# Reordering the tail of a mixture-of-experts stage: bias matmuls, sums' loads, residual chunks and a wait for key rows

## The reference

```
xn = layernorm(x); s = mixer_l(xn); g = silu(ffn_l(xn)); x = x + s * g
```

## Time and profile before

| what | value |
|---|---|
| runs before | 835.33, 833.63, 836.16 us; median 835.33 us |
| profiled execution | 835.67 us, of which the span is 833.9 us; mean granted TensorE clock 0.954 |
| busy, share of the span | PE 84%, DVE 77%, ACT 61%, POOL 47% |
| chain that ended last, by engine | PE 34%, DVE 22%, issue 18%, POOL 13%, ACT 10%, DMA 3% |

### The profile page before, as it was taken

The page is one execution under the profiler, slowest core; times in us unless marked ns, Lnnn a source line. Parts: engine busy times, 40 slices in busy tenths (PEclk is TensorE's granted clock), DMA queues, the critical chain, the costliest instruction groups (busy, mean ns, idle before and its releaser), DMA issues.

```text
span 833.9 us, 13257 instructions
## 1 busy us (share of the span) xinstructions
PE 702.1 (84%) x4706; PEld 352.3 (42%) x4720; DVE 643.3 (77%) x1290; ACT 507.6 (61%) x746; POOL 388.3 (47%) x385
## 2 busy tenths in 40 slices
PE   5996987989979977869999989994877888888986
PEld 2332453444446753334444444441323344444453
DVE  3988777888727745787989924489899999899995
ACT  4788645888865545626666653668454555555473
POOL 0000305686836652041000002028999999999962
PEclk9996997999999996987999999997999999999999
DMA  8600000000144119100000000305447444645441
GB/s 348 277 1 0 4 1 1 1 31 23 37 117 132 44 28 298 42 0 2 3 2 3 2 2 1 126 16 166 159 154 276 147 149 143 201 162 178 156 161 51
DMA packets 30433, 75.97 MB, mean 91 GB/s; under 512 B 4335, under 2 KB 14008, under 8 KB 29344
## 3 DMA queue, kind: packets, MB, share of 16 engines
q1 hardware_dynamic: 26048, 67.41, 23.7%
q0 software_dynamic: 4320, 7.72, 2.7%
HBM read 59.28 MB, written 17.01 MB: 91 GB/s over the span
## 4 chain that ended last, share of the span: by engine, by line
PE 34%; DVE 22%; issue 18%; POOL 13%; ACT 10%; DMA 3%; SPq 0%; DVEq 0%; POOLq 0%; ACTq 0%
POOL arena L2231 7%; PE ps L806 4%; DVE ttr_out L960 4%; DVE xq L960 4%; DVE arena L2156 3%; DVE band L2163 3%; POOL exp_in L2198 3%; PE ps L784 2%; PE ps L642 2%; PE ps L295 2%; PE ps L1448 2%; ACT arena L876 2%; PE ps L652 1%; PE ps L772 1%; PE ps L1215 1%
## 5 line engine op out<-in xcount | busy, mean ns | idle before, releaser
L2156 DVE TENSOR_TENSOR_SCAN arena<-ps,arena 128x1024 f32<-128x1024 f32 x64 | 146.6, 2291 | 18.5 <-ACT ps L2032 9.8
L876 ACT ACTIVATE arena<-ps 128x1024 f32<-128x1024 f32 x128 | 124.8, 1025 | 35.3 <-PE ps L795 25.8
L2032 ACT ACTIVATE ps<-arena,negA 128x1024 f32<-128x1024 f32 x64 | 71.5, 1118 | 102.0 <-DVE arena L2156 101.7
L1866 PE MATMUL ps<-band,w 128*128 128x512 f32 x256 | 120.1, 592 | 0.0
L2163 DVE TENSOR_TENSOR band<-arena,ps 128x1024 f32<-128x1024 f32 x64 | 76.6, 1196 | 2.3 <-PE ps L1751 2.3
L2231 POOL TENSOR_TENSOR arena<-arena,gate 128x1024 f32<-128x1024 f32 x32 | 75.6, 2366 | 4.3 <-DMA gate<-b_dram 3.4
L2231 POOL TENSOR_TENSOR arena<-arena 128x1024 f32<-128x1024 f32 x32 | 75.2, 2364 | 0.3
L806 PE MATMUL ps<-arena 128*32 128x256 f32 x1024 | 70.9, 397 | 1.0 <-ACT arena L876 1.0
L1751 PE MATMUL ps<-xq,sel 128*128 128x512 bf16 x115 | 35.7, 383 | 41.8 <-DVE band L2163 39.1
L1074 POOL COPY arena<-arena 128x128 f32<-128x128 f32 x32 | 8.4, 296 | 123.7 <-PE ps L806 107.2
L1866 PEld LDWEIGHTS ps<-band,w 128*128 128x128 f32 x256 | 48.6, 190 | 40.2 <-issue 30.6
(11 more groups left out here) (404 smaller groups left out, 1620.4 us busy)
## 6 DMA issues: line engine op xcount, KB each, us to landing
gate<-b_dram SPq DMA_DIRECT2D x32, 512.0 KB, 3.7
arena<-b_dram SPq DMA_DIRECT2D x32, 512.0 KB, 4.4
wf<-pack1f_dram SPq DMA_DIRECT2D x1, 3076.0 KB, 15.2
wf<-bias_rows SPq DMA_DIRECT2D x1, 3072.0 KB, 15.4
exp_in<-band SPq DMA_DIRECT2D x2, 1032.0 KB, 5.0
exp_out<-band SPq DMA_DIRECT2D x2, 1024.0 KB, 17.9
e_in<-band SPq DMA_DIRECT2D x2, 1024.0 KB, 21.7
arena<-e_out SPq DMA_DIRECT2D x4, 512.0 KB, 5.7
```

What stands on the lines that cost most here:

```text
L876: act.activation(probs[g % 2][:, 2 * pr:2 * pr + 2, :, :].rearrange("p h k n -> p (h k n)"), PAIRS[l][("S2", i, b)], ACT.Exp).then_inc(A[" ...
L1866: mm = pe.matmul(ps[:, j, :], ident, hc[i % 2][:, j * CH:(j + 1) * CH], start=False, stop=True, skip_group_check=True)
L2032: act.activation(dA_ps, dt3[:, cb, hf * HALF:(hf + 1) * HALF], ACT.Exp, scale=negA[:, cb * STATE + n:cb * STATE + n + 1]).then_inc(M["dA"], 1)
L2156: dve.tensor_tensor_scan(hst[i % 2], dA_ps, dbu[i % 4], 0.0, ALU.mult, ALU.add).then_inc(M["scan"], 1)
```

## The change

The bias matmuls move behind the last `down`. SP issues the four loads of the sums before it waits for `rows_ready`. DVE takes each residual two sums behind its own sum, so that the list reads sum 0, sum 1, sum 2, residual 0, sum 3, residual 1, residual 2, residual 3. In block 2's attention DVE's wait for all 256 of `k_rows` moves from before the order to each key eviction (before it stands a wait for 64, which block 1 has met). In block 3 the second early projection moves behind the logits.

```
-            dve.wait_ge(k_rows, 16 * HH * (1 if l == 1 else 4))
+            dve.wait_ge(k_rows, 16 * HH)
...
                     dve.wait_ge(*A.at("rep_ps", n + 1))
+                    dve.wait_ge(k_rows, 16 * HH * (1 if l == 1 else 4))
                     dve.tensor_tensor(k_st[:, g, c * CH:(c + 1) * CH], ...k_pat, ALU.add)
...
-                if j == N1:
-                    bias_from_table()
                 if 1 <= j <= N1:
                     turn(j - 1)
                 if j >= 2:
                     down(j - 2)
+            bias_from_table()
...
-            for c in range(NCH):
+            def sum_of(c):
                 dve.wait_ge(*MOE.at("y_in%d" % c, 16))
                 a_, b_ = (y1[k][:, 4 * c:4 * c + 4, :] for k in range(2))
                 dve.tensor_tensor(a_, a_, b_, ALU.add).then_inc(MOE["y_sum"], 1)
+            for c in range(NCH + 1):
+                if c < NCH:
+                    sum_of(c)
+                if c >= 2:
+                    residual_dve(dve, 1, ..., (c - 2,))
+            residual_dve(dve, 1, ..., (NCH - 1,))
...
                 if t == NT // 2:
                     project(0, 0, 0)
-                    project(1, 0, 1)
...
             mm.then_inc(M["lg"], 1)
+            project(1, 0, 1)
             project(2, 1, 0)
...
+            moe_sums(sp_)
             sp_.wait_ge(rows_ready, 1)
             sp_.dma_start(bias_rows..., rows_sb...).then_inc(rows_out, 16)
-            moe_sums(sp_)
             sp_.wait_ge(rows_out, 16)
...
             moe_dve(dve)
-            residual_dve(dve, 1, lambda c: chunk(s_sb, c), lambda c: [MOE.at("acc", c + 1)])
```

More of the change, by code:

```diff
@@ L1542, in moe_dve @@
                 dve.tensor_tensor(a_, a_, b_, ALU.add).then_inc(MOE["y_sum"], 1)
+            for c in range(NCH + 1):
+                if c < NCH:
+                    sum_of(c)
+                if c >= 2:
+                    residual_dve(dve, 1, lambda c: chunk(s_sb, c), lambda c: [MOE.at("acc", c + 1)], (c - 2,))
+            residual_dve(dve, 1, lambda c: chunk(s_sb, c), lambda c: [MOE.at("acc", c + 1)], (NCH - 1,))
         def moe_pool(pool):
```

## The result

The changed kernel takes 830.16 us (median of 12 runs, 828.12 to 835.03) against 835.4 us for the kernel before in the same runs: 0.9939, 95% interval 0.9925 to 0.9953. Run a second time it gave 0.9952 (0.9932 to 0.9971). So the change brings 4 to 5 us where 2.0 were forecast. Its profiled execution took 830.28 us with a span of 828.4 us, at a mean granted clock of 0.956.

What follows compares the result with a forecast made beforehand. Scatter, loads, sums and norm, then a later-ending DMA chain to the key rows, were taken as the bound. Gains of 1.1 (first key eviction) and 0.9 (projection) made 2.0 us: 833.7 profiled, 833.3 median, range 830.6 to 837.0.

Steps and rivals of the forecast that it cites:

- The two chains: Before block 2's key evictions: scatter, loads, sums, norm; and DMAs alone (bias write, `bias_q`, near tables, key rows), ending later.
- Bias matmuls behind the last tile: At the last expert tiles: the last scatter starts 1.36 us earlier, limited by POOL running scatters back to back.
- `rows_ready` and the loads first: Before the sums: `rows_ready` stays at about 310.1, and issuing the loads ahead of the write takes nothing off the sums.
- The write behind the loads: In the sums' DMA queue: the bias rows' write lands at 319.8, 0.2 us after the fourth load.
- The restart of `bias_q`: After the bias write: the emptied queue makes `bias_q` take 11.3 us, landing at 331.3, 1.5 later than before.
- Residuals chunk by chunk: At sums and norm: sum 3 starts 0.6 us late, yet PE starts the norm 1.0 earlier.
- The wait moved: Block 2's attention: low halves end by 336.2, key rows land at 338.8, and the first key eviction gains 1.1 us.
- The projection: Block 3: one projection less ahead of the last logits starts routing 0.9 us sooner, carried to the end.
- the clock that falls while PE waits: Rival, chance 0.11: PE's idling before R5 halves the clock, R5 to F0 costs 4.2 us more; 837.5 to 841.
- The first rival: Chance 0.17: the bias write mixes with the loads or the restart is cheap; R1 gains 2.6 to 3.7; 830.7 to 831.8.

Runs made afterwards that it cites:

- two experiments: Changed kernel with the wait for all key rows back ahead of the order, 836.57 us; kernel before with only block 3's projection moved, 834.89 us.

## Why the prediction was wrong

The two chains, their order and the waits are there as forecast. The total is wrong by one step that failed, one size, and a term that was left out. From the tile to DVE's last instruction the changed kernel gains 525.88 - 522.70 = 3.2 us: 2.1 at R1, 0.9 at the projection, and 0.2 in between, where no edit lies. Another 3.63 - 2.54 = 1.1 come behind it: 4.3 us in all, a ratio of 0.9949, which lies in both measured intervals. What stands ahead of the tile, 1.15 us of the two profiled spans' difference, is not the change. The second pair of profiles gives 526.53 - 524.44 = 2.1, with the end's 1.1 only 3.2, since block 3 began at half clock in the changed kernel. Of the 2.3 us that the first pair has above the forecast 2.0, 1.1 are the end, 1.0 are R1 and 0.2 lie in between.

- **Bias matmuls behind the last tile: right.** Predicted 1.36 earlier for the last scatter, measured 5.34 - 4.07 = 1.27. POOL does run back to back: 307.27 - 305.96 = 1.31.
- **`rows_ready` and the loads first: this step failed.** "So `rows_ready` stays at about 310.1" is 5.75 from the tile; it came at 308.23 + 1.10 = 309.33, 6.13 from it, because ACT had to wait for the bias matmuls behind the last `down` (1.54 us ahead of 308.04). And the sum kept the 2.58 us that the last scatter had taken with the write beside it, although the write now goes out behind the loads, and these behind the scatter. The scatter landed 2.08 after its issue, 6.15 from the tile. That is also the moment of `rows_ready`, so that "this edit takes nothing off the sums" fell as well: with the write ahead of them the loads go out at 6.64 and 6.65, without it at 6.30. Predicted were 6.71. That it is the write that delays the scatter is likely and not shown: the five profiles with the write beside it have 2.57 to 2.58, the nine others 2.08, but those five are also the ones with the bias matmuls in their old place.
- **The write behind the loads: right.** It landed 0.2 after the fourth load (15.00 and 14.78 from the tile), as predicted.
- **The restart of `bias_q`: right in kind, 0.5 too dear.** 10.8 us from issue to landing, 11.3 predicted. (The 1.37 for 512 KB in that sum stands in no row; with the 1.32 of rows 3 it would be 11.2.) Together with the loads, `bias_q` landed 25.80 from the tile instead of the predicted 331.3 - 304.35 = 26.95, and the key rows 7.6 behind it. That is why R1 gained 2.1 and not 1.1.
- **Residuals chunk by chunk: right.** Sum 3 ran 0.7 behind its data (0.6 predicted), and the norm's first matmul stood behind its transposes, 1.56 earlier where 1.0 was predicted; 0.4 of the difference is the loads'. The last low half ended at 30.79 from the tile (31.85 predicted). As forecast, none of that reaches R1, which waits for key rows.
- **The wait moved: right**, with an idle stretch of 2.70 ahead of R1 (2.6 predicted) and nothing lost from R1 to the first scores. "Without the moved wait the change would lose here" held as well (R1 at 36.30, 35.57 before).
- **The projection: right in five profiles of eight.** 0.86 where 0.9 was predicted; in the three with half clock at the start of block 3 it loses 0.93 instead. No step looked at what the move does to the clock there. The times pull both ways: the run of the move alone leaves at most 0.3 us for it, the run without it 1.3 or 2.4.
- **Left out: the end of the kernel.** The added waits lengthen DVE's list, and that moves a transfer of instructions out of the last store's way: 1.1 us (3.2 us for the store in the kernel before, 2.1 in the same kernel with 24 more waits). No step of the prediction looked at what a longer list does, and the row for it, 3.2 us for the last store where the median of the four is 2.1, was in the trace before.

Of the rivals, the clock that falls while PE waits did not come in the changed kernel (1.00 from 336 to 342). It did in two experiments (0.59 from 338.5 to 342, 0.57 from 338 to 342), at 0.9 and 1.5 us, where 4.2 had been named. The first rival, a write that overtakes the loads or a cheap restart, named 830.7 to 831.8, next to the measured 830.16. That is mostly luck: the write did not overtake the loads, the restart was 0.5 cheaper, R1 gained 2.1 and not the 2.6 to 3.7 that went with those times, and the end made up the difference.

## What to carry to other kernels

Work out again when each semaphore comes after an edit, ahead of pricing the next edit by it, and ask of each duration that you carry over what ran beside it: `rows_ready` came only 0.4 later, and the write's new place went with a scatter of 2.08 instead of 2.58 and loads that go out 0.35 earlier. An edit that adds entries to an engine's list can move a transfer of instructions: here 1 more entry in DVE's list put one 2.6 us earlier and 24 more entries 24.4 us earlier, counted from the last store's issue, and the store took 2.1 us instead of 3.2. So compare the DMAs at the very end of the span before putting a gain of 1 us down to the edit itself. And where a part's worth is under 1 us and single runs spread over 3 to 9, read it from rows, counted from a mark that stands ahead of the change, and from several profiles: one profile of the projection's move shows a gain of 0.86, the next one a loss of 0.93.

## What was not expected of the hardware

**A transfer of instructions beside a store.** The five profiles with the 8 KB transfer during the last store show 3.2 us for its 256 KB, the nine others 2.1. The transfers of instructions on queue 8 have 16 KB each (38 packets, 0.62 MB), those on queue 14 have 8 KB (27 packets, 0.22 MB). The transfer starts 1.83 behind the last store's issue with 1600 entries in DVE's list, 0.80 ahead of it with 1601, and 22.4 to 22.6 ahead with 1624, in every profile of the kind: as it would if it hung on DVE's place in its list; whose instructions it brings is not shown. In the packets' record it takes 0.31 us, and the store's last packet starts as it ends, 2.14 behind the issue instead of 1.65. The landing follows that packet by 1.05 instead of 0.45; why, is not shown.

**The clock's place moves from run to run.** PE idles 6.4 to 9.0 us ahead of the first sum's transposes in all 14 profiles and then runs at 0.50 for at least 2 us. How far that stretch reaches into the norm differs:

```profile
308.00:322.50 14.50, 6.42 (x20) 4.05 (x20) 7.03 (x11) 4.94 (x8) 0.24 (x1) 0.53 0.68 219
```

```profile
308.00:326.50 18.50, 8.52 (x25) 4.73 (x26) 7.46 (x12) 5.69 (x9) 1.94 (x2) 0.54 0.73 246
```

The first row is the changed kernel, the second the kernel before, each from the end of the experts to where its clock is back up (1.00 from 322.5 to 326 and from 326.5 to 336). From the norm's first matmul to its first product it takes 5.42 in the one and 5.94 in the other, and 6.59 in the changed kernel with the write first. Such differences of 0.5 to 1.8 us stood in the norm, at R, in the scores and at the start of block 3, also between profiles of one kernel. Four profiles with PE idle for 2.7 to 2.9 us ahead of R5 kept the clock at 1.00 there; one with 2.8 ahead of R0 (0.57 from 338 to 342) and the one with 4.76 (0.59 from 338.5 to 342) did not. These differences are likely why the times of one kernel spread over 3 to 9 us, and why 1.2 to 1.8 us won at R1 by another order of issues can't be seen in the time; that they make up the whole spread is not shown, as one run in each set was profiled. What decides a run's share of them stays open.
